# Two denominators of the gates formed by chained DMAs, with new orders on four engines

## What is computed

```
forget_gate = sigmoid(x @ W_f.T + b_f);  input_gate = sigmoid(x @ W_i.T + b_i)
gate_sum    = forget_gate + input_gate + EPS            # EPS = 1e-8
forget_norm = forget_gate / gate_sum;  input_norm = input_gate / gate_sum
new_info    = input_norm * (x @ W_h.T + b_h)
log_cumprod = cumsum(log(forget_norm + EPS), axis=1)
scaling     = exp(log_cumprod[:, -1:] - padded[:, :-1])   # product over the later steps
hidden      = cumsum(scaling * new_info, axis=1) + exp(log_cumprod) * cond
x1          = x + hidden
h_t         = tanh(x1_t @ Wx + b + h_{t-1} @ Wh);  out = x1 + h
```

## Time and profile before

| | |
|---|---|
| median of the runs | 194.7 us |
| the profiled execution, its time | 194.83 us |
| its span, first to last instruction | 193.0 us |
| TensorE busy | 180.9 us (94%) |
| VectorE busy | 131.7 us (68%), 292 instructions |
| ScalarE busy | 115.4 us (60%) |
| GpSimd busy | 24.4 us (13%) |
| `denominator`, line 409 | 8 instructions, 9.7 us |
| chain that ended last | TensorE 53%, VectorE 23%, ScalarE 14% |

### The profile page before, as it was taken

How to read it: one execution, slowest core, us unless ns; L and a number is a source line. 1 busy time by engine, 2 the same in 40 slices (tenths; PEclk the granted TensorE clock), 3 DMA queues, 4 the chain that set the end, 5 groups by cost and what they waited for, 6 DMA issues and landing times.

```text
span 193.0 us, 3133 instructions
## 1 busy us (share of the span) xinstructions
PE 180.9 (94%) x1178; PEld 161.4 (84%) x1178; DVE 131.7 (68%) x292; ACT 115.4 (60%) x235; POOL 24.4 (13%) x28
## 2 busy tenths in 40 slices
PE   6799999999999995999989999999999999999990
PEld 6678878888888884787879989999999999999880
DVE  0044569999998999999999999795999520200121
ACT  3309998996996897162223264656556565645550
POOL 1000000200100011131011210222211222221000
PEclk9999999999999998899999999999999999999998
DMA  5994340750320019299003035625374473627326
GB/s 112 246 250 115 109 109 19 171 138 3 59 51 0 0 33 184 41 190 192 15 5 54 5 49 93 128 41 131 51 153 69 77 141 56 135 38 154 59 48 169
DMA packets 12910, 17.83 MB, mean 92 GB/s; under 512 B 2080, under 2 KB 10720, under 8 KB 12896
## 3 DMA queue, kind: packets, MB, share of 16 engines
q0 software_dynamic: 4960, 7.87, 24.8%
q1 hardware_dynamic: 6848, 9.77, 19.5%
q10 hardware_dynamic: 1088, 0.00, 0.3%
HBM read 5.57 MB, written 4.19 MB: 51 GB/s over the span
## 4 chain that ended last, share of the span: by engine, by line
PE 53%; DVE 23%; ACT 14%; issue 5%; DMA 2%; SPq 0%; DVEq 0%
PE ps L932 29%; PE ps L903 9%; DVE suf L445 6%; DVE den L409 3%; PE ps L941 3%; PE ps L911 3%; ACT den L289 3%; DMA x_rows<-in_x 2%; PE ps L790 2%; ACT L278 2%; PE ps L796 2%; DVE q_s L430 2%; PE ps L792 2%; PE ps L781 2%; DVE q_s L419 2%
## 5 line engine op out<-in xcount | busy, mean ns | idle before, releaser
L932 PE MATMUL ps<-h_t,wh_f 128*128 128x128 f32 x504 | 69.3, 278 | 1.0 <-ACT h_t L309 0.7
L309 ACT ACTIVATE h_t<-ps,bias 128x64 f32<-128x64 f32 x128 | 37.2, 314 | 49.1 <-PE ps L932 43.7
L932 PEld LDWEIGHTS ps<-h_t,wh_f 128*128 128x128 f32 x504 | 62.2, 191 | 4.4 <-ACT h_t L309 3.3
L790 PE MATMUL ps<-x_hi,wt_lo 128*128 128x512 f32 x96 | 38.8, 404 | 3.1 <-DVE q_s L457 2.1
L792 PE MATMUL ps<-x_hi,wt_hi 128*128 128x512 f32 x96 | 38.2, 398 | 0.0
L796 PE MATMUL ps<-x_lo,wt_hi 128*128 128x512 f32 x96 | 30.3, 398 | 0.0
L243 POOL DMA_DIRECT2D den<-h_t x14 | 16.7, 1191 | 73.4 <-ACT h_t L309 73.4
L790 PEld LDWEIGHTS ps<-x_hi,wt_lo 128*128 128x128 f32 x96 | 18.3, 191 | 7.6 <-issue 3.9
L796 PEld LDWEIGHTS ps<-x_lo,wt_hi 128*128 128x128 f32 x96 | 18.5, 194 | 4.3 <-DVE x_lo L395 0.3
L792 PEld LDWEIGHTS ps<-x_hi,wt_hi 128*128 128x128 f32 x96 | 18.3, 191 | 3.6
L445 DVE SCALAR_TENSOR_TENSOR suf<-r_d,suf 128x128 f32<-128x128 f32 x64 | 18.5, 290 | 1.8
(11 more groups left out here) (62 smaller groups left out, 232.3 us busy)
## 6 DMA issues: line engine op xcount, KB each, us to landing
x_rows<-in_x SPq DMA_DIRECT2D x16, 256.0 KB, 4.2
x_lo<-x_hi POOLq DMA_DIRECT2D x8, 512.0 KB, 5.2
den<-h_t POOLq DMA_DIRECT2D x14, 256.0 KB, 3.8
out_x<-x_rows SPq DMA_DIRECT2D x14, 256.0 KB, 3.2
out_x<-x_rows SPq DMA_DIRECT2D x2, 192.0 KB, 2.7
h_t<-in_L_cond_W_f SPq DMA_DIRECT2D x1, 256.0 KB, 4.8
h_t<-in_L_cond_W_i SPq DMA_DIRECT2D x1, 256.0 KB, 6.1
h_t<-in_L_cond_W_h SPq DMA_DIRECT2D x1, 256.0 KB, 7.4
```

The lines of the kernel that those rows point to most:

```text
L309: nc.scalar.activation(h_t[:, c % 2, a, cols(t)], ps[:, 4 * (c % 2) + 2 * a + t % 2, cols(t // 2)], ACT.Tanh, bias=bias[:, 3, a:a + 1])\
L790: last = nc.tensor.matmul(to, w_lo[:, dk, rows], x_hi[:, c, dk], start=dk == 0, stop=False, skip_group_check=True)
L932: return nc.tensor.matmul(bank[:, :, cols(t // 2)], wh_f[:, dk, a * P:(a + 1) * P], twice, start=False, stop=dk == 1, skip_group_check=True)
```

## The change

For n = 3 and n = 5 the denominator isn't formed on VectorE. When the forget gate is there, SP copies it into the slot of `den` by a DMA; when that has landed and the input gate is there, GpSimd issues a DMA that adds the input gate; when that has landed, ScalarE takes Ln with EPS as its bias. The two DMAs of a chunk follow one another, each waited for by its semaphore. On GpSimd these stand in front of the `whole_x`, whose order is changed: chunks 0 to 3 first, 4 to 7 behind the output sums of chunks 0 to 3. On SP the copy for n = 3 stands between the loads of x chunks n = 6 and n = 7.

The orders on VectorE, ScalarE and TensorE are changed too. The instructions in them are the same but for `denominator(3)` and `denominator(5)`, which are gone, and a memset of one column. The diff, with blank lines and unchanged stretches left out:

```diff
 NATIVE = 2
+DEN_BY_DMA = (3, 5)
 EPS = 1e-8
...
         first = sb("first", [P, 1])
+        eps = sb("eps", [P, 1])
...
         den_ready = sem("den_ready")
+        den_copied = [sem(f"den_copied{n}") for n in range(NCH)]
+        den_summed = [sem(f"den_summed{n}") for n in range(NCH)]
         ln_ready = sem("ln_ready")
...
             sp.dma_start(wh_f[:, :, :], wh.rearrange("(a p) d -> p a d", p=P)).then_inc(wh_landed, 16)
+            def copy_forget(n):
+
+                sp.wait_ge(gate_ready, 4 * n + 2)
+                if n >= RING:
+                    sp.wait_ge(i_inv_ready, n - RING + 1)
+                    sp.wait_ge(u_ready, n - RING + 1)
+                sp.dma_start(den[:, n % RING], r_d[:, chunk_of(n) + 1]).then_inc(den_copied[n], 16)
+
             for n in range(2, NCH):
...
                 load_x(n)
+                if n - 3 in DEN_BY_DMA:
+                    copy_forget(n - 3)
+            for n in range(NCH - 3, NCH):
+                if n in DEN_BY_DMA:
+                    copy_forget(n)
             for c in range(NCH - 1):
...
-            for c in CAND_ORDER:
+            def add_input_gate(n):
+
+                pool.wait_ge(den_copied[n], 16)
+                pool.wait_ge(gate_ready, 4 * n + 4)
+                nc.gpsimd.dma_start(den[:, n % RING], q_s[:, chunk_of(n)], accum_op=ALU.add)\
+                    .then_inc(den_summed[n], 16)
+
+            for n in DEN_BY_DMA:
+                add_input_gate(n)
+            for c in range(4):
                 whole_x(c)
...
                     out_sum(c, th)
+                if c + 4 < NCH:
+                    whole_x(c + 4)
...
                 for k in group:
-                    act.wait_ge(den_ready, k + 1)
-                    nc.scalar.activation(den[:, k % RING], den[:, k % RING], ACT.Ln).then_inc(ln_ready, 1)
+                    if k in DEN_BY_DMA:
+                        act.wait_ge(den_summed[k], 16)
+                        act.wait_ge(ones_ready, 2)
+                        nc.scalar.activation(den[:, k % RING], den[:, k % RING], ACT.Ln, bias=eps[:, 0:1])\
+                            .then_inc(ln_ready, 1)
+                    else:
+                        act.wait_ge(den_ready, sum(n not in DEN_BY_DMA for n in range(k + 1)))
+                        nc.scalar.activation(den[:, k % RING], den[:, k % RING], ACT.Ln).then_inc(ln_ready, 1)
                 for k in group:
...
+            split_w(0)
             split_x(0)
-            split_w(0)
             split_w(1)
             split_w(2)
+            layer1_weight()
+            first_state()
             split_x(1)
...
             split_x(3)
-            layer1_weight()
-            first_state()
             sigmoids(2)
...
             inverses((7,))
+            nc.scalar.preload_act_table_set("sigmoid_and_others")
             move_candidate(4)
             move_candidate(1)
-            nc.scalar.preload_act_table_set("sigmoid_and_others")
             move_candidate(2)
...
                     dve.wait_ge(u_ready, n + 1)
-                    dve.wait_ge(ones_ready, 2)
+                    dve.wait_ge(ones_ready, 3)
                 if n >= SUF and k == 0:
...
             nc.vector.memset(first[:, :], 0.0).then_inc(ones_ready, 1)
+            nc.vector.memset(eps[:, :], EPS).then_inc(ones_ready, 1)
             nc.vector.memset(suf[:, SUF - 1, :, cols(0)], 1.0).then_inc(ones_ready, 1)
...
             chunk_split(1)
+            weight_split(2)
             denominator(0)
             chunk_split(2)
-            i_by_den(0)
             ratio(0)
-            weight_split(2)
-            chunk_split(3)
             denominator(1)
             suffix(0, 7)
+            chunk_split(3)
+            layer1_weight_rest()
+            i_by_den(0)
+            denominator(2)
             suffix(0, 6)
+            chunk_split(4)
             suffix(0, 5)
...
             suffix(0, 3)
-            denominator(2)
-            chunk_split(4)
             suffix(0, 2)
             suffix(0, 1)
+            ratio(1)
             suffix(0, 0)
-            by_suffix(0)
-            product(7)
-            ratio(1)
-            ratio(2)
             suffix(1, 7)
...
             suffix(1, 2)
-            layer1_weight_rest()
+            i_by_den(2)
             suffix(1, 1)
             chunk_split(5)
+            ratio(2)
+            by_suffix(0)
             suffix(1, 0)
...
             suffix(2, 6)
-            by_suffix(1)
             suffix(2, 5)
...
             suffix(2, 3)
+            denominator(4)
             suffix(2, 2)
+            by_suffix(1)
+            chunk_split(6)
+            product(7)
+            ratio(3)
             suffix(2, 1)
-            denominator(3)
-            denominator(4)
-            chunk_split(6)
-            i_by_den(2)
             suffix(2, 0)
-            ratio(3)
-            i_by_den(3)
+            by_suffix(2)
             suffix(3, 7)
             suffix(3, 6)
-            i_by_den(4)
             suffix(3, 5)
+            i_by_den(3)
             suffix(3, 4)
             suffix(3, 3)
-            chunk_split(7)
+            i_by_den(4)
             suffix(3, 2)
-            denominator(5)
             suffix(3, 1)
...
             suffix(4, 7)
-            by_suffix(2)
+            chunk_split(7)
             suffix(4, 6)
             suffix(4, 5)
-            denominator(6)
             suffix(4, 4)
...
             suffix(4, 2)
+            denominator(6)
             suffix(4, 1)
+            suffix(4, 0)
             product(6)
-            suffix(4, 0)
-            i_by_den(5)
+            product(5)
             ratio(5)
...
             suffix(5, 7)
-            denominator(7)
+            i_by_den(5)
             suffix(5, 6)
-            product(5)
             suffix(5, 5)
...
             suffix(6, 7)
+            denominator(7)
             suffix(6, 6)
...
             suffix(6, 4)
+            suffix(6, 3)
             i_by_den(6)
-            suffix(6, 3)
             suffix(6, 2)
+            ratio(7)
             suffix(6, 1)
-            ratio(7)
+            i_by_den(7)
             suffix(6, 0)
...
             suffix(7, 4)
-            i_by_den(7)
             suffix(7, 3)
...
             product_first(0)
+            by_suffix_first(1)
             chain(0, 0, 4)
             plus_decay(0, 0)
-            by_suffix_first(1)
+            product_first(1)
+            first_layer(0, 0)
+            chain(0, 4, 8)
             by_suffix(6)
-            first_layer(0, 0)
-            product_first(1)
+            plus_decay(0, 1)
             moved_product(1)
-            chain(0, 4, 8)
+            first_layer(0, 1)
             chain(1, 0, 4)
-            plus_decay(0, 1)
+            chain(1, 4, 8)
             plus_decay(1, 0)
-            first_layer(0, 1)
-            chain(1, 4, 8)
-            product(3)
             plus_decay(1, 1)
             first_layer(1, 0)
+            product(3)
             first_layer(1, 1)
...
             first_layer(4, None)
+            chain(5, 0, 4)
             x1_rest(4, 0)
-            chain(5, 0, 4)
             x1_rest(4, 1)
...
             plus_decay(5, None)
+            first_layer(5, None)
             chain(6, 0, 4)
             chain(6, 4, 8)
-            first_layer(5, None)
             chain(7, 0, 4)
...
             plus_decay(6, None)
+            plus_decay(7, None)
             first_layer(6, None)
-            plus_decay(7, None)
+            x1_rest(6, 0)
             first_layer(7, None)
-            x1_rest(6, 0)
             x1_rest(6, 1)
...
                                  skip_group_check=True)
+            transpose_w(0)
             transpose_x(0)
-            transpose_w(0)
+            gates(0, 0)
             transpose_w(1)
-            gates(0, 0)
+            transpose_w(2)
             transpose_x(1)
-            transpose_w(2)
             transpose_cond()
...
             transpose_x(6)
-            candidate(1)
             gates(5, 0)
             gates(5, 1)
+            candidate(1)
             transpose_x(7)
...
             gates(7, 0)
+            candidate(2)
             gates(7, 1)
-            candidate(2)
             candidate(3)
...
             candidate(5)
```

## The result

The changed kernel took 195.92 us in the median of 20 runs, 194.70 to 198.39. The kernel before took 194.63 us in 20 runs, 194.11 to 195.14. The ratio is 1.006, with a 95% interval of 1.0043 to 1.0077: slower by over 0.3%, where 193.1 and faster had been forecast. (The ratio leaves out three executions that took over 1.5% more than the fastest; the median and the spread do not.) Two things are in these numbers. The best executions are level with before (194.7), so the expected gain of 1.6 us is missing.

The account below looks back on a forecast made before the run. VectorE was taken to set the recurrence's start, by the end of first_layer(1, 1). Gains of 1.35 there and 0.2 at the start, 1.6 us, took 194.7 to 193.1 us; forecast 192.3 to 194.0 (0.50), range 191.6 to 195.4.

Parts of the forecast that it names:

- The start: TensorE's first work, weight 0 transposed ahead of x chunk 0: gates(0, 1) 0.2 us earlier, bounds -0.5 and +0.5.
- What goes: Two of eight denominator instructions leave VectorE: 2 x 1.14 = 2.28 us.
- The wait at `ratio(1)`: VectorE reaches ratio(1) at 35.7 and stands idle 1.5 us for chunk 1's inverse, losing most of the saved 2.28 us.
- The walk from 37.2 on: VectorE's instructions counted by price list to by_suffix_first(0) at 84.5, 1.2 us earlier; first_layer(1, 1) ends at 102.45.
- The DMA path: Copy 4.4 us plus addition 4.8 us, 9.2 us in series before Ln; VectorE doesn't wait for chunks 3 and 5.
- Rival A: Both chained denominator DMAs land late before Ln: gain eaten at 10.1 us, 196.1 us at 10.8; chance 0.17.
- rival B: Only chunk 3's copy is late, beside an x load: VectorE waits 1.2 us at ratio(3), time 194.3 us; chance 0.13.
- Moves at no cost: SP's last x load, four whole_x behind output sums and chunk_split(7) come later, covered by existing waits: no cost.
- The sum: 1.35 us from the earlier recurrence plus 0.2 at the beginning, 1.6 us gained: 194.7 to 193.1 us.
- The third rival: No starvation: ratio(1) finds its inverse ready or the 1.5 us are filled otherwise, time 191.6 us; chance 0.10.
- a first `gates(0, 1)` later than 14.73: Sign that the forecast is wrong: TensorE's gates(0, 1) starts later than the 14.73 us of the kernel before.
- a wait in the recurrence for a `whole_x`: Sign that the forecast is wrong: a whole_x transfer moved behind the output sums is waited for in the recurrence.

Follow-up runs that it names:

- experiment 5: The changed kernel with the order of the kernel before at the start on TensorE and ScalarE: 194.52 us, ratio 0.9999.
- experiment 6: The kernel before with only the change's start on TensorE and ScalarE (weight 0 ahead of x chunk 0): 195.31 us, ratio 1.0075.
- experiment 7: The changed kernel with 12 warm-up products on TensorE in place of 9: 194.94 us, ratio 1.0023.
- experiment 8: The changed kernel with the denominators of chunks 3 and 5 formed on VectorE again, none by DMA: 198.0 us, ratio 1.0189.
- experiment 9: The kernel of experiment 5 with by_suffix(0) moved ahead of ratio(1) and ratio(3) moved behind by_suffix(2) on VectorE: 192.89 us, ratio 0.9895 against the kernel before.
- experiment 1: The changed kernel with GpSimd's whole_x put back early, behind the denominator DMAs, none among the output sums: 195.45 us, ratio 1.0076.
- experiment 3: The changed kernel with first_layer(6) ahead of plus_decay(7) on VectorE, as in the kernel before: 194.82 us, ratio 1.0038.
- experiment 4: The changed kernel with semaphores of the DMA denominators for chunks 3 and 5 only, 4 in place of 16: 195.42 us, ratio 1.0064.
- experiment 10: The kernel of experiment 9 with first_layer(6) ahead of plus_decay(7) on VectorE: 193.16 us, ratio 0.9913 against the kernel before.
- experiment 2: The kernel before with only GpSimd's whole_x order taken from the change: 194.36 us, ratio 0.9992.

## Why the prediction was wrong, step by step

**The start** is the largest step that failed. The prediction costed the new order of TensorE's first work at a gain of 0.2 us, with bounds of 0.5 to either side, by counting matmuls. It left out TensorE's wait for weight 0, whose 4.9 us of landing end at 6.9 where x chunk 0 was there at 5.97. The profile before showed this landing, for a transfer issued at 2.00 (the last figure is us from issue to landing):

```profile
h_t<-in_L_cond_W_f SPq DMA_DIRECT2D x1, 256.0 KB, 4.8
```

It also left out that TensorE may not have reached its higher level when it runs out of work. Experiments 5 to 7 show that both losses are the start's. Against the profiled execution before, the new start cost 0.36 us (`gates(0, 1)` at 15.09) where 0.2 had been entered as a gain: 0.56 us of error; against before in general it costs 0.7 (experiment 6). In the executions that stay at 1.2 GHz until about 14 us it costs 2.4 us more. The median of 195.92 lies 0.9 us above the profiled 195.0 through such executions, as the scatter goes with the old start or with 12 warm-up products; but the ten times between 195.3 and 196.5 and the highest, 3.4 us above the profiled one, were not caught in a trace, so how they arise isn't shown. No rival held any of this: the cases were all about DMAs and VectorE. The bound of 0.5 us rests on no row, only on the uncertain order of landing.

**What goes**, 2.28 us of VectorE's time: right in kind. Experiment 8 gives 1.8 us for it in this order, 2.1 by the spans.

**The wait at `ratio(1)`**: right in place and size (1.5 forecast, 1.42 measured), and experiment 9 confirms what it costs. With it filled, and the 0.50 us below gone too, the median falls 1.6 us from experiment 5's.

**The walk from 37.2 on**: right. The forecast starts were 53.2 for `ratio(3)`, 69.1 for `ratio(5)`, 84.5 for `by_suffix_first(0)`; with the start's 0.4 us these are 53.6, 69.5 and 84.9, against 53.66, 69.93 and 85.33. The 0.4 us on the last two are the 0.50 us ahead of `by_suffix(2)`. VectorE stands there from 55.4 to 55.91, put down to its own suffix step. It is in the traces of the kernel after and of experiments 1, 3, 4, 5 and 7, in some of which VectorE comes to that place 2.3 us later, and not in 8, 9 and 10. So it goes with the program and not with the moment. Its cause wasn't settled.

**The DMA path**: right in effect, though by little, and the two errors in it cancel. The copies took 3.4 and 2.9 us (4.4 forecast), the additions 5.2 and 4.5 (4.8 forecast), and 0.3 us pass between the landing of a copy and the issue of its addition. From the forget gate to the sum of chunk 3 it is 9.0 us (9.2 forecast). Rival A (late DMAs, given 0.17) and rival B (the first copy delayed by the x load, 0.13) are both refuted by the trace: Ln of neither chunk waited. The copy within SBUF was mis-sized from loads out of HBM. Chunk 3's Ln had nothing to spare; VectorE came for its inverse about 0.4 us after it was there.

**Moves at no cost**: wrong for `whole_x`. The last landed after 7.2 us, not 6 to 7 behind a sum, and VectorE waited 3.68 us. The prediction had called this covered by VectorE's idle time, and had not asked what stands behind `plus_decay(7)` on the engine: the change puts `first_layer(6)` there, on which the recurrence depends. It costs 0.2 us at the end of the profiled execution after. In that of experiment 7, where the recurrence is 0.2 us later, it costs nothing, and the best times of experiments 1 and 3, which take away the wait or what it held up, are no lower than the best after (194.75 and 194.72 against 194.70). In the kernel before, with the old order on VectorE, the late `whole_x` costs nothing (experiment 2).

**The sum.** It holds a slip: the end of `first_layer(1, 1)`, forecast at 102.45, was set against the start of TensorE's products before, 103.79, though these had begun 0.15 us after that instruction's end at 103.64. After the change they began 0.14 us behind it too (103.29 and 103.43), so 1.35 us should have read 1.2. For the profiled execution the forecast was 194.83 - 1.6 = 193.2, and it took 195.0. The 1.8 us between are 0.56 at the start, 0.50 at `by_suffix(2)`, 0.14 of this slip, 0.2 in the recurrence and 0.37 outside the span (2.2 less 1.83), which had no term at all: together 1.8. To the median it is 0.9 us more, by the slower start. Of these, the start is the largest; the others, together 1.2 us, are what is missing in experiment 5. The third rival (no starvation, 191.6) didn't occur; its premise, that the 1.5 us can be filled, is what experiment 9 makes use of.

What had been named as a sign of failure did show: "a first `gates(0, 1)` later than 14.73" and "a wait in the recurrence for a `whole_x`". The mechanism of the middle stands. The ends of the kernel were not looked at with the same care.

## What to carry to other kernels

When the first work of an engine is reordered, set the landing time of each input beside the time at which the engine is free; on TensorE an idle microsecond ahead of the first real products can cost more than its length, by chance, if the warm-up has not yet brought it to its higher level. An instruction that may wait should stand behind, not ahead of, those on which the critical engine depends, even on an engine that is half idle. Work taken off a busy engine is worth only what its next wait leaves: look for the instruction that can stand in that wait before moving anything.

## What the runs showed of the hardware

- TensorE did products of 512 columns in 0.63 us or in 0.40 us at the same place of one order in different executions, with a granted clock of 1.00 in both. In the three slow ones it had run its nine warm-up products wholly at the lower level and then stood 1.1 us without work; with twelve the slower level at this place didn't occur in 11 runs.
- In the eleven profiled executions without a slow start TensorE rose to its higher level at 4.4 to 7.2 us, at another time from one to the next. Where it had risen by 4.5 us, 1.7 us without work behind the warm-up did not bring it down (experiments 6 and 8).
- A copy of 512 KB within SBUF from SP's queue lands 2.9 to 3.4 us after issue, an adding transfer of GpSimd of the same size 4.5 to 5.2 us, and directly behind an output sum of GpSimd 5.8 us (three times) and 7.2 us (once).
- Two more transfers of GpSimd lengthened the time outside the span by 0.4 us (1.8 to 2.2, one execution each); two more of SP did not.
